# Counting and weighing of a few-key attention rebuilt, with weight splits moved, in a two-layer transformer kernel

## The reference

```python
Q, K, V = x @ Wq.T + bq, x @ Wk.T + bk, x @ Wv.T + bv      # 16 heads of 16
lam = 10.0 * exp(-5.0 * u_prev); use_sparse = lam >= 1.0   # per batch
# sparse: query s sees the keys idx[s, 0:32], repeats counted, masked ones left out
sparse_out = softmax(Q . K[idx] * scale) @ V[idx]
out = where(use_sparse, sparse_out, dense_out) @ Wo.T + bo
x = x + relu(out @ w1 + b1) @ w2 + b2
h = gelu(x @ fc1.T + f1b); c = concat(h @ fc2.T, h @ experts[b].T)
x = x + top-2 mixture of 8 experts over c
```

## Time and profile before

| | |
|---|---|
| runs | 580.24, 579.69, 577.02 us; median 579.69 |
| profiled execution | span 574.7 us from first to last instruction; a time of its own beside the span is not listed |
| busy | PE 528.6 us (92%), DVE 432.0 (75%), ACT 248.3 (43%), POOL 200.6 (35%) |
| chain that ended last | PE 62%, DVE 23%, issue 6%, ACT 4%, POOL 3% |
| stages | to 7.5 us setup; to 71.4 counting and projections; to 94.1 first guards; to 272.7 attention; to 574.7 dense |

### The profile page before, as it was taken

One profiled execution on the slowest core, in us unless ns is written; L12 is line 12 of the kernel. 1 busy time (PEld: TensorE's weight loads), 2 busy tenths in 40 slices (PEclk: granted clock), 3 DMA queues, 4 the chain that ended last, 5 costly groups with the idle time before them and its releaser, 6 DMA issues.

```text
span 574.7 us, 7798 instructions
## 1 busy us (share of the span) xinstructions
PE 528.6 (92%) x2585; PEld 365.3 (64%) x2585; DVE 432.0 (75%) x923; ACT 248.3 (43%) x516; POOL 200.6 (35%) x318
## 2 busy tenths in 40 slices
PE   4999879899999999889599999999999999999897
PEld 2467645444444444335477887888878888788786
DVE  6699857998998999975478588483884838847286
ACT  5366337677677776774246250042500425003100
POOL 6688547896887977800042000010000100000000
PEclk9999989899999999999699999999999999999989
DMA  7100001110101101000141000100001000010000
GB/s 264 57 1 2 1 1 38 36 37 1 38 2 36 38 1 38 2 1 2 41 123 62 0 2 18 47 10 1 0 19 46 10 0 1 21 46 1 9 10 28
DMA packets 11506, 15.66 MB, mean 27 GB/s; under 512 B 5954, under 2 KB 8258, under 8 KB 11330
## 3 DMA queue, kind: packets, MB, share of 16 engines
q1 hardware_dynamic: 11458, 15.07, 8.3%
HBM read 12.97 MB, written 2.10 MB: 26 GB/s over the span
## 4 chain that ended last, share of the span: by engine, by line
PE 62%; DVE 23%; issue 6%; ACT 4%; POOL 3%; DMA 2%; DVEq 0%; SPq 0%; ACTq 0%; POOLq 0%
DVE shift L825 7%; PE psG L1033 4%; PE psG L1035 4%; PE psG L1034 4%; PE psO L485 4%; DVE Pr L849 4%; PE psM L1033 4%; PE psO L590 3%; PE psM L1034 3%; PE psM L1035 3%; PE psS L1033 3%; PE psS L1035 3%; PE psS L1034 3%; PE psO L1033 3%; PE psO L1035 3%
## 5 line engine op out<-in xcount | busy, mean ns | idle before, releaser
L849 DVE SCALAR_TENSOR_TENSOR Pr<-Pr,W 128x1024 f32<-128x1024 f32 x64 | 88.0, 1381 | 3.6 <-ACT Pr L718 3.3
L825 DVE TENSOR_REDUCE shift<-psG 128x2 f32<-128x512 f32 x116 | 74.4, 681 | 16.3 <-PE psG L556 15.5
L718 ACT ACTIVATE Pr<-psS 128x512 f32<-128x512 f32 x128 | 70.2, 606 | 24.9 <-PE psS L573 24.5
L552 PE MATMUL psG<-KG,QG 128*128 128x512 f32 x116 | 53.1, 500 | 5.9 <-DVE shift L825 3.0
L1156 POOL TENSOR_TENSOR cT_lo<-attT,cT_hi 128x1024 fp32r<-128x1024 f32 x4 | 10.1, 2522 | 134.1 <-ACT cT_hi L1119 134.1
L1143 ACT ACTIVATE V<-psS,cols 128x512 f32<-128x512 f32 x16 | 11.0, 688 | 104.9 <-PE psS L1035 104.9
L573 PE MATMUL psS<-QAT,KP 128*128 128x512 f32 x128 | 49.6, 457 | 5.2 <-ACT Pr L718 5.1
L311 POOL TENSOR_SCALAR EQ_pool<-iota,idx 128x256 f16<-128x256 f16 x48 | 47.5, 1001 | 14.1 <-PE psO L485 8.9
L1180 DVE CAST hT_hi<-V 128x512 fp32r<-128x512 f32 x64 | 34.7, 542 | 15.6 <-ACT V L1140 8.7
L556 PE MATMUL psG<-Mneg,identm 128*128 128x512 bf16 x116 | 46.4, 400 | 0.0
L1182 DVE TENSOR_TENSOR hT_lo<-V,hT_hi 128x512 fp32r<-128x512 f32 x64 | 44.3, 692 | 2.2
(11 more groups left out here) (239 smaller groups left out, 1337.1 us busy)
## 6 DMA issues: line engine op xcount, KB each, us to landing
Pr<-xT_dram SPq DMA_DIRECT2D x1, 2048.0 KB, 9.6
staged<-w_dram SPq DMA_DIRECT2D x4, 512.0 KB, 3.6
x1T<-xT_dram SPq DMA_DIRECT2D x4, 512.0 KB, 4.5
staged<-ew_dram SPq DMA_DIRECT2D x4, 512.0 KB, 3.8
out_dram<-y SPq DMA_DIRECT2D x16, 128.0 KB, 1.7
staged<-fc_dram SPq DMA_DIRECT2D x2, 512.0 KB, 3.6
Pr<-wqkv_dram SPq DMA_DIRECT2D x1, 768.0 KB, 5.0
staged<-fc2a_dram SPq DMA_DIRECT2D x1, 512.0 KB, 3.5
```

The costliest lines, as they stand in the source:

```text
L552: nc.tensor.matmul(o, self.QG[:, (ug // 2) % 2, st * P:st * P + P], self.KG[:, ug % sh.NB, 2 * p:2 * p + 2, blk * 256:blk * 256 + 256], st ...
L718: nc.scalar.activation(Pr[:, n % JOBS, 512 * f:512 * f + 512], psS[:, f, :], ACT.Exp, scale=SCALE).then_inc(self.s["s_exp"], 1)
L825: nc.vector.tensor_reduce(dst, self.guard_bank(gj)[0][:, p, :].rearrange("p (h t) -> p h t", h=2), AX.X, ALU.max, negate=True).then_inc(se ...
L849: nc.vector.scalar_tensor_tensor(pr, pr, FMAX, W[:, r * 1024:r * 1024 + 1024], ALU.min, ALU.mult).then_inc(self.s["s_prob"], 1)
```

## The change

A class `Few` takes the place of `Attention` for 256 keys; `Attention` stays for all keys (not run here). What it does:

- *Counting.* Entries come in as 128 partitions (4 groups of rows by 32 entries) by 256. PE spreads each partition over 32 (8 *spread* steps of 16 matmuls, 256 columns each, four side by side in 32 output rows), ACT copies 1024 columns to fp16 (`idxb`), DVE compares 1024 wide with a key number per partition (64 comparisons in all), and PE adds 32 rows to one (`sum16`, 8 matmuls of 512 columns for 4 comparisons). POOL and ACT compare nothing. Projections stand in steps 3 to 6, five each. ACT stores the counts as `W` (bf16, keys on partitions); PE turns them for `Mneg`.
- *Logarithms.* ACT takes Ln of the counts, DVE scales them by 4 and adds a large negative number where the count is 0, ACT and POOL split them (`LH`, `LL`). In jobs 3 and 7 of 8 the score gets both added by PE (two matmuls more for each half), and DVE's weigh falls away.
- *Shift.* DVE's reduction writes straight into `Qa`, column 48 (one part, not two). ACT and POOL fill `Qa` half a unit at a time (*fill*); query_rows turns two tiles at once.
- *Weights.* fc1 goes from EARLY to LATE: 5 early pieces, 9 late ones (fc1 5 and 6, the three Wc pieces 7 to 9, ew 10 to 13), with a new `LATE_AT`. xT is loaded in two parts.

```diff
+NT, NQ = FEW_KEYS // P, S // P
+STEPS = 8
+KEY_SETS = FEW_KEYS // 32
+EQ_RING = 8
+HALF = NQ // 2
+FILLS = 2 * UNITS
+SLOTS = 3
+LEAD, SPLIT = 4, 6
+PROJ_FROM = 3
+
+ADD_AFTER = (1, 2, 4, 5, 7)
+
+LOGGED = (3, 7)
...
-            nc.vector.tensor_copy(idmf, idm[:, :, :].bitcast(U8)).then_inc(s["self_setup"], 1)
-            nc.vector.tensor_copy(idx1[:, :, :], idx).then_inc(s["self_setup"], 1)
-            dve.wait_ge(s["self_setup"], 2)
-            nc.vector.scalar_tensor_tensor(idx1[:, :, :], idx1[:, :, :], 1.0, idmf,
+            nc.vector.scalar_tensor_tensor(idxm[:, :], idx4[:, :], 1.0, msk4[:, :].bitcast(U8),
                                            ALU.add, ALU.mult).then_inc(s["idx_ready"], 1)
...
-            for b in range(B):
-                nc.vector.tensor_scalar(identm[:, b, :], ident, lam[:, 2, b:b + 1], None,
-                                        ALU.mult).then_inc(s["consts_ready"], 1)
...
+            def opening(self):
+
+                for k in range(2):
+                    yield "spread", k
+                for k in range(STEPS):
+                    for j in (2 * k + 2, 2 * k + 3):
+                        if j < STEPS:
+                            yield "spread", j
+                    if PROJ_FROM <= k < STEPS - 1:
+                        for j in range(len(ADD_AFTER)):
+                            yield "project", (k - PROJ_FROM) * len(ADD_AFTER) + j
+                    if k == STEPS - 1:
+                        yield "guard_keys", 0
+                        yield "fill", 0
+                    yield "count", k
+                yield "counted", 0
+                yield "turn_counts", 0
+                yield "turn_counts", 1
+                yield "logs", 0
...
+                    if (t + 3) % HALF == 0 and 1 <= (t + 3) // HALF < FILLS:
+                        yield "fill", (t + 3) // HALF
...
+                    if 1 <= n <= n_jobs and (n - 1) % JOBS not in LOGGED:
+                        yield "weigh", n - 1
+                    if t >= 4 and t % 2 == 0 and (t - 4) // 2 < n_jobs // 2:
+                        yield "query_rows", (t - 4) // 2
...
+                    if what == "logs":
+                        pool.wait_ge(self.s["log_hi"], 1)
+                        nc.gpsimd.tensor_tensor(self.LL[:, :, :], self.logs, self.LH[:, :, :].bitcast(F32),
+                                                ALU.subtract).then_inc(self.s["log_lo"], 1)
+                    if what == "fill":
+                        pool.wait_ge(self.s["q_hi"], i + 1)
+                        q, qa = self.query_halves(i)
+                        nc.gpsimd.tensor_tensor(qa[:, :, :, 32:48], q, qa[:, :, :, 0:16].bitcast(F32),
+                                                ALU.subtract).then_inc(self.s["q_lo"], 1)
...
+                        flat = self.spread_bank(i)[:, :, :].rearrange("p a b -> p (a b)")
+                        for qq in range(4):
+                            for j in range(4):
+                                p0 = i * 16 + qq * 4 + j
+                                mm = nc.tensor.matmul(flat[32 * j:32 * j + 32, qq * 256:qq * 256 + 256],
+                                                      ident16[:, p0:p0 + 1].to_broadcast([P, 32]),
+                                                      idxm[:, :], start=True, stop=True, tile_position=(0, 32 * j))
+                        mm.then_inc(self.s["bc_full"], 1)
...
+                    if what == "count":
+                        for tt in range(NT):
+                            e = i * NT + tt
+                            pe.wait_ge(self.s["eq_ready"], 4 * (e + 1))
+                            bank = psS if tt else psG
+                            for f in range(2):
+                                for j in range(4):
+                                    mm = nc.tensor.matmul(bank[32 * j:32 * j + 32, f, :], self.sum16[:, :],
+                                                          self.EQ[:, (4 * e + j) % EQ_RING, 512 * f:512 * f + 512],
+                                                          start=(i == 0), stop=(i == STEPS - 1), tile_position=(0, 32 * j))
+                            mm.then_inc(self.s["eq_used"], 1)
...
+                                mm = nc.tensor.matmul(flat[:, a:a + P], self.W[:, tt, q0:q0 + P], self.identb[:, :],
+                                                      start=True, stop=True)
...
+                        for f in range(2):
+                            if i == 0:
+                                pe.wait_ge(self.s["g_max"], 2 * LAG)
+                            else:
+                                pe.wait_ge(self.s["s_exp"], 2 * (i - 1) + f + 1)
+                            q = slice(512 * f, 512 * f + 512)
+                            mm = nc.tensor.matmul(psS[:, f, :], self.KP[:, u % 2, j, r * P:r * P + P],
+                                                  self.QAT[:, u % 2, j // 2, q], start=True, stop=not logged)
+                            if logged:
+                                nc.tensor.matmul(psS[:, f, :], self.ident32[:, :], self.LL[:, r, q], start=False, stop=False)
+                                mm = nc.tensor.matmul(psS[:, f, :], self.ident32[:, :], self.LH[:, r, q], start=False, stop=True)
+                            mm.then_inc(self.s["s_scores"], 1)
...
+                        pe.wait_ge(self.s["s_exp"], 2 * HG * (i + 1))
+                        pe.wait_ge(self.s["s_prob"], weighed_before(HG * (i + 1)))
...
+                nc.scalar.copy(self.identb[:, :], ident).then_inc(self.s["consts"], 1)
+                nc.scalar.copy(self.ident32[:, :], ident).then_inc(self.s["consts"], 1)
+                nc.scalar.copy(self.sum16[:, :], sum32).then_inc(self.s["consts"], 1)
...
+                    if what == "spread":
+                        act.wait_ge(self.s["bc_full"], i + 1)
+                        nc.scalar.copy(self.idxb[:, i, :],
+                                       self.spread_bank(i)[:, :, :].rearrange("p a b -> p (a b)")).then_inc(self.s["bc_out"], 1)
+                    if what == "counted":
+                        for tt in range(NT):
+                            act.wait_ge(self.s["eq_used"], STEPS * NT - NT + 1 + tt)
+                            bank = psS if tt else psG
+                            nc.scalar.copy(self.W[:, tt, :], bank[:, :, :].rearrange("p a b -> p (a b)")).then_inc(self.s["w_out"], 1)
+                    if what == "logs":
+                        act.wait_ge(self.s["atleast1"], 1)
+                        nc.scalar.activation(self.logs, self.marks, ACT.Ln).then_inc(self.s["ln_out"], 1)
+                        act.wait_ge(self.s["log_ready"], 1)
+                        nc.scalar.copy(self.LH[:, :, :], self.logs).then_inc(self.s["log_hi"], 1)
+                    if what == "fill":
...
+                    if what == "count":
+                        for g in range(KEY_SETS):
+                            e = i * KEY_SETS + g
+                            if g == 0:
+                                dve.wait_ge(self.s["bc_out"], i + 1)
+                            if e >= EQ_RING and g % 4 == 0:
+                                dve.wait_ge(self.s["eq_used"], (e - EQ_RING) // 4 + 1)
+                            nc.vector.tensor_scalar(self.EQ[:, e % EQ_RING, :], self.idxb[:, i, :], keyno[:, g:g + 1], None,
+                                                    ALU.is_equal).then_inc(self.s["eq_ready"], 1)
+                            if PROJ_FROM <= i < STEPS - 1 and g in ADD_AFTER:
+                                projected((i - PROJ_FROM) * len(ADD_AFTER) + ADD_AFTER.index(g))
+                    if what == "turn_counts":
+                        dve.wait_ge(self.s["turned_full"], i + 1)
+                        nc.vector.tensor_scalar(Mneg[:, i * S:(i + 1) * S], psO[:, :, :].rearrange("p a b -> p (a b)"),
+                                                0.0, -BIG, ALU.is_equal, ALU.mult).then_inc(self.s["neg_out"], 1)
+                        if i == 0:
+                            nc.vector.tensor_scalar(self.marks, self.W[:, :, :], 1.0, None, ALU.max).then_inc(self.s["atleast1"], 1)
+                    if what == "logs":
+
+                        dve.wait_ge(self.s["ln_out"], 1)
+                        nc.vector.tensor_scalar(self.marks, self.W[:, :, :], 0.0, -BIG, ALU.is_equal,
+                                                ALU.mult).then_inc(self.s["none_ready"], 1)
+                        dve.wait_ge(self.s["none_ready"], 1)
+                        nc.vector.scalar_tensor_tensor(self.logs, self.logs, 1.0 / SCALE, self.marks, ALU.mult,
+                                                       ALU.add).then_inc(self.s["log_ready"], 1)
...
+                            nc.vector.tensor_reduce(self.Qa[:, f % SLOTS, st, 2 * p:2 * p + 2, 48],
+                                                    self.guard_bank(i)[0][:, p, :].rearrange("p (h t) -> p h t", h=2), AX.X,
```

(12 more changed lines are left out.)

689 lines of the change are left out of this document (530 added, 159 removed).

## The result

The changed kernel takes **573.92 us** (median of 13 runs, 573.06 to 575.55), the old one 579.52 (median of 13 beside them, 574.94 to 581.41): ratio 0.9933, interval 0.9913 to 0.9952, so 0.67% faster. Forecast was 567.5. The time of a run lies about 2 above its span in both kernels; the profiled run of the old kernel (574.7) was one of its fastest, that of the changed one (573.0, time 575.06) lay 1.1 above its median.

A forecast was written before the change was run, and what follows sets the result against it. DVE was taken as the attention's bound, at 22.2 us a unit, with PE not far behind. 574.7 - 18.6 - 3 + 1.5 + 7.9 = 562.5, plus 5.0 to the median: 567.5 us, range 553 to 580.

The forecast's parts named there:

- Part 3: Attention unit: DVE loses two weighs, PE takes over as the bound; 21.7 against 22.2 a unit, 3 us gained.
- Part 1: Counting: comparisons of 0.40, PE the later side in steps 3 to 6; last comparison ends at 49.3, counting had ended at 71.4.
- rival (b): Counting: the comparison runs at the fp32 rate, 0.67 each, 12 us more, 579.5; chance 0.08.
- Part 2: From counts to first score: a 9.6 us chain, then guards in 16.6 as before; first score 18.6 us earlier.
- Rival (c), lockstep,: Attention: PE only one guard ahead of DVE, each turn costs the longer side; unit 24.7, +19.5, 587; chance 0.12.
- slack argument: Attention, against lockstep: followed turn by turn with one guard of slack, DVE is free again whenever PE's next guard is ready.
- Part 4: Last twelve scores: three logged jobs add 12 matmuls, 2.8, three weighs fall away; half shows, 1.5 us lost.
- Part 5: Dense part: late weight pieces slip two places and form a chain; cT_lo ends at 309.0, 7.9 us lost with lower clock.
- The idle time that I had named as a sign: Dense part: PE idle for several us before ao of chunk 1, from about 304, released by cT_lo.
- Rival (a): Dense part: the chain doesn't bite because loads landed earlier than 5.0 after issue; 559.6; chance 0.12.
- Fewer early splits gain nothing: Attention: splitting fewer weight pieces early brings no gain, since those splits lay beside DVE.
- The step to the median: Whole kernel: the median of the runs lies 5.0 above the profiled execution's span, so 562.5 becomes 567.5.

The follow-up runs named there:

- Run 11: Changed kernel with no logarithms at all: not computed in the opening, no jobs logged: 556.3 us, ratio 0.9621 to the old kernel.
- runs 4 to 6: Changed kernel with the logged jobs moved from 3 and 7 to 1 and 5, 0 and 4, 2 and 6: 561.85, 562.63 and 569.46 us.
- run 1: Changed kernel with no logged jobs, all eight weighed by DVE, logarithms still computed: 564.63 us, ratio 0.9768 to the old kernel.
- run 3: Changed kernel with only the high part of the logarithm added to the scores, low part left out of the result: 566.38 us, ratio 0.98.
- run 12: Changed kernel without any logarithms and with fc1 split early as in the old kernel (seven early, seven late pieces): 555.6 us, ratio 0.9597.
- run 16: Changed kernel with 32 unused bytes put ahead of Wo, w1 and w2: 577.23 us, ratio 0.9986 to the old kernel.
- runs 12 and 13: The second: changed kernel without logarithms, fc1 split early, high parts of early weights copied at guard 7: 551.98 us, ratio 0.9553. The first: see run 12.
- runs 16 and 18: The second: changed kernel with Wo, w1 and w2 moved on by 64 bytes: 576.95 us, ratio 0.9982. The first: see run 16.
- run 7: Changed kernel with the low parts of the early weight pieces computed on DVE in place of POOL: 574.84 us, ratio 0.9938.

## Why the prediction was wrong

The sign was right and the size was not: 5.6 gained where 12.2 was forecast. **The step that failed is Part 3**, the unit of the attention: forecast 21.7, so 3 gained; measured 24.6 (the mean of five, 101.4 to 224.5), so 11.7 lost over seven units. PE's row was put too short, and the added matmuls stand where the relief of DVE gives nothing back. The mechanism of the opening held with one overlap wrong in it, and the dense part came out 9.2 better than forecast, which hid most of the error of Part 3.

**Part 1 held.** A comparison takes 0.40 as taken from the earlier trace rows, so rival (b) is out, and in steps 3 to 6 DVE waits for PE's projections (1.83 at 23.4, 1.50 at 36.8). The first comparison came at 9.04 (forecast 10.0), the memset beside the second cost 1.7, the last ended at 51.1 (49.3; the forecast's own terms, 19.6, 24.2 and 2, give 45.8 and not 46.1 on the way). A memset on POOL was nowhere in my sum. The Trainium skill (SBUF — State Buffer, SBUF: two separate sides) says that the port pair which GpSimd shares with VectorE's two-port modes is an exclusive lock, held for a whole instruction, while the loser waits; by that rule the memset and a comparison in such a mode can't overlap. The trace agrees: 2.16 beside 2.09.

**Part 2, two terms.** The chain was right in length (9.2, forecast 9.6). That `LH` and `LL` "end near 66 and are hidden under the twelve guards" is the sentence that failed: `LL` ended at 67.0 and took 4.55, about as costed, but I asked only who waits for `LL`, not what is queued behind it on POOL. With the table load, which I left out, the guards took 19.2 for 16.6. Run 11 has 16.5 with the cause gone. In sum 15.3 earlier and not 18.6.

**Part 3.** I put PE at 19.1 in the old kernel, well under DVE's 21.7, and so gave the change 2.7 of room before PE became the bound. The old kernel's windows show 21.5 busy, level with DVE's 21.3. Not all of the 2.4 between is work. With jobs 1 and 5 logged the changed kernel's 127 matmuls show 22.6 busy, so without the eight added ones (1.9) the row is 20.7 at most. That makes my sum up to 1.6 too short, and the 21.5 and 23.4 hold waits. My sum took each kind at its best pace inside a run of its like: a plain score at 2 x 0.233 = 0.47, where 0.54 pass from it to the next guard (186.88 to 187.42 in the rows above) and more when its second half waits for an exp; some 21 small transposes at 0.11. I had the check in hand: PE's busy time in the earlier trace rows, 134.6 of 144.6, is 20.7 a unit, and I went by my own sum. The second error is the overlap: with jobs 3 and 7 the turns behind the logged scores are PE's anyway, so that DVE's two weighs less gave nothing back (table of runs 4 to 6), and 1.5 of each unit stayed beyond PE's busy time, where I had left 0.7. The third is what run 1 leaves: 3.6 of the attention that have nothing to do with the logged jobs.

**Rival (c), lockstep,** had the size of the unit, 24.7 against 24.6, and saw that the place counts; I gave it 0.12 on a slack argument followed. Runs 4 to 6 show that the place is worth 12 of the time. Its turns are not those measured, though: it has 3.3 for the logged one and 1.8 behind it, where 3.95 and 2.74 passed, so the equal size is in part luck, and a time of 587 it missed with the rest of the sum. Both causes act: the added matmuls in full (run 3), and the place.

**Part 4** held: 1.5 forecast, 3.2 measured, of which 1.6 is the stretch at the lower clock.

**Part 5: three terms, two not in the sum.** The late chain did cost, 4.3 by run 12, and from h 2 to the end of `cT_lo` 26.7 in place of 22.6; forecast 7.9. The wait of y 0 was 3.16 (forecast 2.4), but `cT_lo` ended at 302.7, not 309.0, and PE, at y until 303.2, went on to ao of chunk 1 without a wait: 4.0 of the 6.3 is the earlier start of h 2, and the load of piece 8 took 4.4 from its first issue to its split (285.09 to 289.50), where I took 5.7. The idle time that I had named as a sign is hidden in this trace, since PE ran at the lower clock in y 0 (first window); in run 16's, which has that clock later, it shows (second row):

```profile
293.40:300.20 6.80, 6.17 (x15) 4.81 (x16) 3.67 (x5) 2.71 (x3) 2.25 (x1) 0.50 0.47 154
```

```profile
301.31 0.52 PE L1545 MATMUL psS<-cT_lo,Wo_hi 128*128 128x512 f32 x1 [2.25 <-POOL cT_lo L1668]
```

In all the first output comes 77.7 after the attention, was 76.5: 4.8 of chain less 3.6 of the gap after the attention that fell away. After that matmuls were faster, 2.5 (from the first output to the last 220.8, was 223.3). Rival (a), which lets the dense part lose nothing, comes near the measured -1.3 for another reason. And "Fewer early splits gain nothing" failed: two of them are worth about 2 (runs 12 and 13).

**The step to the median.** I added 5.0 to the span of the profiled run. It was a low run of a kernel whose runs scatter over 6.5; those of the changed one scatter over 2.5, and its median is 0.9 above the profiled span. So 4.1 of an error of 10.5 in the spans were hidden, and 6.4 was left. Much of the old kernel's scatter goes with its granted clock: of its 67 runs beside the experiments, the 7 with a mean of 0.988 took 574.1 to 576.8, the 22 with 0.979 took 577.9 to 580.7. Why its clock varies more from run to run than the changed kernel's isn't settled.

## What to carry to other kernels

Before you trust a sum by kinds of instruction, hold it against the busy time of the same engine in the same window; where it comes out lower, the engine may already be the bound, and then a gain elsewhere is worth nothing while each added instruction counts in full. Busy time is the upper end, since it can hold waits. Where two engines run one or two buffers apart, the place of a long piece of work counts as much as its length: ask whether the relieved engine is the one waited for in the very turn in which the relief falls, and try the other places before giving the change up (here 12 of 574 us, by two numbers). And of a new piece of work on a quiet engine ask what is queued behind it, not only who waits for it.

## What the runs showed of the hardware

- **Matmul pace by the place of the weights.** In a y job 128x512 matmuls follow each other every 0.229 or every 0.235 to 0.236 (10.77, 11.05 and 11.09 for 47 steps) at a granted clock of 1.00. In the changed kernel it goes by where the weights lie in memory, and is worth about 3 in a dense part of 300 (303.5 and 303.8 in runs 16 and 18, 300.7 in the changed kernel); the old kernel has the slower pace at all three places tried. The Trainium skill (TensorE: Matmul & The Clock Gate, Wait — 56ns, not 53.3ns?) gives 215.7 ns from start to start for 512 columns at the full clock. None of these jobs reached that figure, and the measurement decides.
- **A gap that goes with the place of the code.** After the branch behind the attention PE stood still for 8.2 in the old kernel and for 4.5 in the same kernel with its code 64 instructions further on.
- **The same stall costs or doesn't, by what is queued behind it.** Weighs of 3.2 in place of 1.2 beside a split on POOL stood in four units of the changed kernel; with the splits on DVE three of the four were as long as before (run 7). One of 2.56 beside `KG`, with norm queued behind it, left PE waiting for 1.30.
- **"Busy" holds waits.** PE shows 23.3 to 23.5 busy a unit with jobs 3 and 7 logged, and 22.5 to 22.9 with 1 and 5, for the same 127 or 128 matmuls.
- **The lower clock falls at other places in other runs.** 3.4 at a granted clock of 0.50 stood in the last part of the changed kernel's attention and made it 1.6 longer than in run 7, whose granted clock there was 1.00. A stage's length in one trace is compared only after a look at its granted clock.
